# Score chain one step later, and coordinates spread by DMA instead of TensorE, in a deformable-attention kernel

## Chip, cores and metric

The kernel runs on one core of a Trainium2 chip. The metric is device time in microseconds (us) of one execution. A core has TensorE (PE; its weight loads are listed as PEld), VectorE (DVE), ScalarE (ACT), GpSimd (POOL) and a queue for DMAs (SP, SPq). They run their own instruction streams and meet at semaphores.

## What is computed

The reference applies two layers to an image x of 2 x 128 x 32 x 32. Each layer is deformable attention with 8 heads and a continuous position bias, and an MLP:

```python
q = _gconv1x1(xn, qw)
off = conv(qg, off_dw_w, stride 4, 6x6);  off = gelu(off + off_dw_b)
off = tanh(einsum(off, off_pw_w)) * OFF_SCALE
vx, vy = gx + off[:, 0], gy + off[:, 1]          # 64 sampling points per head
kv = _grid_sample(xn, (nx, ny));  k, v = _gconv1x1(kv, kw), _gconv1x1(kv, vw)
pos = grid_q[:, :, None, :] - grid_kv[:, None, :, :]
bias = sign(pos) * log1p(abs(pos))
bias = relu(bias @ cpb_w1 + cpb_b1);  bias = relu(bias @ cpb_w2 + cpb_b2)
bias = bias @ cpb_w3 + cpb_b3
attn = softmax(q @ k.T * scale + bias);  x = x + out_w @ (attn @ v) + out_b
return x + mlp_w2 @ gelu(mlp_w1 @ bn(x) + mlp_b1) + mlp_b2
```

The bias MLP runs for each of 2 x 8 x 1024 x 64 query-key pairs and is most of the work.

## The kernel before

**Tiling.** A segment is one layer of one image (4 segments). Each has 4 units (pairs of heads), a unit has two halves of the queries (32 phases in all), and a phase has 8 steps: 256 steps, 64 per segment. In a step the bias MLP is run for one slice of keys:

- VectorE makes the first hidden layer, h1 (L600, one operation over 128 x 2048, three buffers deep).
- TensorE adds the y part and the bias into PSUM ("corrections", L798, 4 products) and runs layer 2 (L824, 16 products). Both fill two of three PSUM pairs.
- ScalarE empties each pair by a relu (L452, two per step).
- TensorE runs layer 3 (L842) into the scores. In the last step of a phase the queries' product with the keys is added (L853).

**The ring.** The three PSUM pairs go round: whoever comes next takes the one that was freed first. The function `ring` settles this when the program is built. Side work that needs PSUM takes its turn too: it takes the pair of the second relu of the step before, and must wait for that relu. The next step's layer 2 then takes the pair of the side work and must wait until that is emptied. Side work that uses the ring is: q, image_t, offset, spread, sample, keys_values, scores_t, attend, project, mlp_up, mlp_down, u_rows. `max_off` writes to the scores and does not.

**What sets the order.** Tables of numbers say after which step a stage stands in the stream of its engine. On TensorE it stands behind layer 2 and before layer 3 of that step. On ScalarE it stands behind both relus. On VectorE it stands behind h1 of that step, which runs up to three steps ahead. `BEFORE_SLOTS` prepares the next segment, at steps 28 to 51 of the running one. `AFTER_SLOTS` finishes a half: attention output, projection, MLP. `SOFTMAX_SLOTS` is the chain of each phase.

**The chain of a phase.** In the step after its last one (number 1 of the next phase) ScalarE copies the scores to SBUF (`copy_scores`, L462). At 2 TensorE transposes them (`scores_t`, L932); `score_max` on VectorE (L727) takes the maxima; `widen_max` on ScalarE (L540) spreads them; `max_off` (L938) subtracts them; `exp` (L546) follows, with a table load where another function stood before.

**Preparation.** ScalarE's `conv_gelu` (step 33), TensorE's `offset` (L892) and ScalarE's tanh give offsets. `positions` on VectorE makes `coord`, with one row per key, and `pos`. Then `spread` (L901) multiplies a broadcast column of `coord` with the identity, 8 times, so that each partition has all keys' coordinates. `spread_out` on ScalarE (L509, L510) reads it into `hat_x` (as a distance) and `key_y` (a part of the tile `work`). `features` (L498 to L503) prepares the bias input. `distances` (L516, 4 pairs), `hats` and `hat_products` on VectorE and GpSimd build the bilinear weights. `sample` (L913) samples the image, and `keys_values` gives keys and values, which `keys_values_out` on ScalarE copies (L530, L532).

**SP.** SP stores the features, loads them broadcast for each unit (L368), and spreads the reciprocals of the softmax sums by a store and a broadcast load (`invert_sums`, L345), which VectorE's divide (L741) awaits.

## Time and profile before

| | us |
|---|---|
| median of 3 runs | 909.36 (906.27 to 911.7) |
| the profiled execution, whole | 908.36 |
| its span in the trace | 906.3 |
| PE busy | 814.3 |
| DVE busy | 711.1 |
| ACT busy | 675.8 |
| PE idle before the score transposes (L932) | 21.5 |

A row of the timeline gives the start, the duration, the engine, the line and the operation, with the tile written and the tiles read. In brackets stands how long the engine was idle before it, and who ended the wait. Rows of the same kind are merged (x4, x16). Matmuls are pipelined, so the last row before a wait ends a little before its modelled end. A busy TensorE is not one at its peak.

### The profile page before, as it was taken

Reading aid. Unit: us, or ns where it says so; the run is one execution under the profiler, and the core shown is the slowest. Engines: PE = TensorE matmul, PEld = TensorE weight load, DVE = VectorE, ACT = ScalarE, POOL = GpSimd, SP = SyncE. Lnnn points to the kernel's source line nnn. Section 1 sums busy time; section 2 is a strip of 40 time slices with the busy share of each in tenths; the row PEclk is TensorE's granted clock in tenths of the full one; section 3 lists DMA queues with packets and bytes.
Section 4 is the critical chain, followed back from the end, with each engine's and each line's share of the span. In section 5 each row is a group of like instructions: output and inputs, shape, how many; then the busy total and the mean of one; then the engine's idle time right before and its main releaser. Section 6 shows DMA issues by size and latency. Waiting matters only on the chain.

```text
span 906.3 us, 27727 instructions
## 1 busy us (share of the span) xinstructions
PE 814.3 (90%) x12452; PEld 229.1 (25%) x12452; DVE 711.1 (78%) x493; ACT 675.8 (75%) x773; POOL 69.1 (8%) x40
## 2 busy tenths in 40 slices
PE   3299998899999999789999999888999999999986
PEld 2122222222222222223222222222222222222222
DVE  4799798798877588888885879889887758989821
ACT  2368787978786688896876878897877768888862
POOL 2110021210000004030000001220000000000000
PEclk8589998999999999999999999999999999999999
DMA  4401010020120102002020100102011010200001
GB/s 150 95 15 48 5 31 21 8 53 4 25 44 12 50 3 50 8 3 55 2 64 14 48 4 26 27 7 54 4 34 40 8 50 2 71 5 2 2 15 36
DMA packets 23781, 27.06 MB, mean 30 GB/s; under 512 B 15600, under 2 KB 17520, under 8 KB 23664
## 3 DMA queue, kind: packets, MB, share of 16 engines
q1 hardware_dynamic: 23664, 25.29, 10.4%
q8 instruction: 99, 1.62, 0.7%
q14 instruction: 18, 0.15, 0.1%
HBM read 23.05 MB, written 2.10 MB: 28 GB/s over the span
## 4 chain that ended last, share of the span: by engine, by line
issue 58%; PE 26%; POOL 6%; ACT 5%; DVE 3%; DMA 0%; ACTq 0%; SPq 0%; POOLq 0%
PE pair L824 9%; PE scores L842 8%; POOL conv_prod L325 4%; POOL big L432 3%; ACT h L452 3%; PE pair L798 2%; DVE h L600 2%; PE pair L975 2%; PE scores L853 1%; PE pair L950 1%; PE pair L932 1%; PE pair L966 1%; ACT big L554 1%; PE scores L938 1%; ACT L554 0%
## 5 line engine op out<-in xcount | busy, mean ns | idle before, releaser
L600 DVE TENSOR_TENSOR h<-hx,hy 128x2048 f32<-128x2048 f32 x256 | 582.3, 2302 | 77.5 <-PE pair L824 73.3
L452 ACT ACTIVATE h<-pair 128x1024 f32<-128x1024 f32 x512 | 517.3, 1023 | 148.0 <-PE pair L798 104.8
L824 PE MATMUL pair<-h,wts 32*32 32x512 f32 x8192 | 301.2, 605 | 21.3 <-DVE h L600 6.7
L842 PE MATMUL scores<-h,wts 128*32 128x512 f32 x2048 | 275.7, 607 | 0.1
L798 PE MATMUL pair<-fy,u_rows 32*128 32x512 bf16 x1024 | 102.8, 388 | 16.6 <-DMA fy<-fy_dram 16.6
L824 PEld LDWEIGHTS pair<-h,wts 32*32 32x32 f32 x8192 | 66.3, 103 | 83.3 <-ACT h L452 35.3
L798 PEld LDWEIGHTS pair<-fy,u_rows 32*128 32x128 bf16 x1024 | 26.3, 91 | 234.2 <-issue 234.2
L842 PEld LDWEIGHTS scores<-h,wts 128*32 128x32 f32 x2048 | 42.1, 108 | 157.0 <-issue 148.5
L325 POOL TENSOR_TENSOR conv_prod<-qpad,wts 128x288 f32<-128x288 f32 x16 | 34.0, 2150 | 416.3 <-ACT qpad L479 416.3
L432 POOL TENSOR_TENSOR big<-big,hat_x 128x512 f32<-128x512 f32 x16 | 32.4, 2054 | 127.7 <-DVE big L698 127.7
L462 ACT ACTIVATE probs<-scores,wts 128x512 f32<-128x512 f32 x32 | 22.0, 688 | 23.8 <-PE scores L842 23.5
L932 PE MATMUL pair<-const,probs 128*128 128x128 f32 x128 | 20.1, 280 | 21.5 <-ACT h L452 20.8
L727 DVE TENSOR_REDUCE neg_max<-pair 128x8 f32<-128x512 f32 x32 | 22.1, 690 | 21.3 <-PE pair L932 21.3
L756 DVE SCALAR_TENSOR_TENSOR x<-pair,wts,x 128x512 f32<-128x512 f32 x8 | 6.0, 751 | 36.9 <-PE pair L975 36.9
L853 PE MATMUL scores<-qpad,keys_t 128*32 128x512 f32 x256 | 33.3, 592 | 0.0
L966 PE MATMUL pair<-work,wts 128*128 128x512 f32 x64 | 31.0, 612 | 1.9 <-DVE work L750 1.4
L975 PE MATMUL pair<-big,wts 128*128 128x512 f32 x64 | 29.5, 604 | 3.0 <-ACT big L554 2.9
L554 ACT ACTIVATE big<-pair,wts 128x512 f32<-128x512 f32 x32 | 20.2, 683 | 15.7 <-PE pair L966 15.6
L932 PEld LDWEIGHTS pair<-const,probs 128*128 128x128 f32 x128 | 13.4, 140 | 49.7 <-issue 48.0
L546 ACT ACTIVATE probs<-scores,wts 128x512 f32<-128x512 f32 x32 | 21.9, 685 | 3.0 <-PE scores L938 2.8
L938 PE MATMUL scores<-ident_r,neg_max_wide 128*128 128x128 f32 x128 | 22.9, 302 | 0.6 <-ACT neg_max_wide L540 0.6
L938 PEld LDWEIGHTS scores<-ident_r,neg_max_wide 128*128 128x128 f32 x128 | 17.2, 190 | 24.7 <-ACT neg_max_wide L540 16.5
(89 smaller groups left out, 358.5 us busy)
## 6 DMA issues: line engine op xcount, KB each, us to landing
hx<-features_dram SPq DMA_DIRECT2D x64, 128.0 KB, 2.8
hy<-features_dram SPq DMA_DIRECT2D x64, 128.0 KB, 3.2
att_den<-reciprocals_dram SPq DMA_DIRECT2D x8, 256.0 KB
wts<-weights_dram SPq DMA_DIRECT2D x2, 960.0 KB, 7.7
x<-x_dram SPq DMA_DIRECT2D x2, 512.0 KB, 5.5
fy<-fy_dram SPq DMA_DIRECT2D x64, 6.0 KB
fy<-fy_dram SPq DMA_DIRECT2D x64, 4.0 KB
fy<-fy_dram SPq DMA_DIRECT2D x64, 2.0 KB
```

The costliest lines, as they stand in the source:

```text
L325: return engine.tensor_tensor(out, window, taps, ALU.mult)
L432: pool.tensor_tensor(bilinear[:, k], hat_y[:, k], hat_x[:], ALU.mult).then_inc(bilinear_ready[0], 1)
L452: emptied("z", 2 * g + j, act.activation(h2[j][g % H2_BUFS][:].rearrange("p r n -> p (r n)"), pair_of("z", 2 * g + j)[:], ACT.Relu))
L600: dve.tensor_tensor(h1[g % H1_BUFS][:].rearrange("p c (y x) -> p c y x", x=W), hx[unit % 2][:, :, t].unsqueeze(2).broadcast_to([128, CT, H ...
L798: return pe.matmul(z_of(g, r), u_rows[unit // PAIRS // B][key_rows(r)], y.unsqueeze(2).broadcast_to([32, H // 2, W]), **flags)
L824: ins = pe.matmul(z_of(g, r)[32 * c:32 * (c + 1)], w(l, "w2")[key_rows(r), key_rows(r)], h1[g % H1_BUFS][key_rows(r), c], start=r >= 2, st ...
L842: ins = pe.matmul(scores[phase % 2][32 * r:32 * (r + 1)], w(l, "w3")[:, 32 * t:32 * (t + 1)], h2[rows[0] // 2][step % H2_BUFS][:, r % 2], ...
L853: ins = pe.matmul(scores[phase % 2][k], keys_t[seg % 2][:, u, k], qpad[seg % 2][:, 1 + H // 2 * h:1 + H // 2 * (h + 1), 1:W + 1], start=Fa ...
L932: ins = pe.transpose(pair_of("scores_t", phase)[:, s], probs[:, unit % PAIRS, bank(h)][:, s], cst("ident"))
L938: ins = pe.matmul(scores[phase % 2][:, 128 * k:128 * (k + 1)], neg_max_wide[:, 2 * k:2 * (k + 1)].rearrange("p n j -> p (n j)"), ident_r[: ...
L966: ins = pe.matmul(pair_of("mlp_up", n)[:, bank(k)], w(half // 2 // B, "mlp_w1")[:, 128 * c:128 * (c + 1)], xn2[:, bank(half % 2)], start=T ...
L975: ins = pe.matmul(pair_of("mlp_down", half)[:, 0:HALF], w(half // 2 // B, "mlp_w2")[:, 128 * c:128 * (c + 1)], mlp_h[:, c, bank(half % 2)] ...
```

## The change

1. In `SOFTMAX_SLOTS` and `AFTER_SLOTS` all numbers grow by one: `scores_t`, `score_max`, `widen_max`, `max_off`, `exp`, and everything that finishes a half.
2. For segments 1 to 3 `spread` and `spread_out` are gone. SP stores column 3 of `coord` (1,024 numbers of 4 bytes) to `coords_dram`, and after the store of the features it loads them back, broadcast over 128 partitions, into `hat_x` and `key_y` (256 KB each). ScalarE makes `hat_x` a distance in place (`hat_x_distance`). Segment 0 keeps the products.
3. In `BEFORE_SLOTS` offset, positions, features and features_sign move by one step, distances, hats and hat_products by three, sample, sample_out and keys_values by four. q, image_t and the convolution stay.
4. The second `u_rows` moves from step 20 to 22.

```diff
-    ("dve", "conv_sum", 1): 34, ("act", "conv_gelu", 0): 33, ("pe", "offset", 0): 35,
-    ("act", "offset_tanh", 0): 35, ("dve", "positions", 0): 38, ("pe", "spread", 0): 37,
-    ("act", "features", 0): 37, ("act", "spread_out", 0): 37, ("dve", "features_sign", 0): 40,
-    ("act", "distances", 0): 39, ("act", "distances", 1): 40, ("act", "distances", 2): 41,
+    ("dve", "conv_sum", 1): 34, ("act", "conv_gelu", 0): 33, ("pe", "offset", 0): 36,
+    ("act", "offset_tanh", 0): 36, ("dve", "positions", 0): 39, ("act", "features", 0): 38,
+    ("dve", "features_sign", 0): 41, ("act", "hat_x_distance", 0): 41, ("act", "distances", 0): 42,
...
-SOFTMAX_SLOTS = {("pe", "scores_t"): 2, ("dve", "score_max"): 4, ("act", "widen_max"): 3,
-                 ("pe", "max_off"): 4, ("act", "exp"): 4}
+SOFTMAX_SLOTS = {("pe", "scores_t"): 3, ("dve", "score_max"): 5, ("act", "widen_max"): 4,
+                 ("pe", "max_off"): 5, ("act", "exp"): 5}
...
+            def store_coords(seg):
+
+                sp.wait_ge(pos_ready, seg + 1)
+                sp.dma_start(coords_dram[seg].rearrange("n k -> k n"), coord[:, 3], allow_slow_non_contiguous=True)\
+                    .then_inc(coords_stored, 16)
+
+            def load_coords(seg):
+                for k in range(2):
+                    sp.wait_ge(bilinear_ready[k], 4 * seg)
+                sp.wait_ge(coords_stored, 16 * seg)
+                for dst, n in ((hat_x[:], 0), (key_y, PAIRS)):
+                    c = coords_dram[seg, n]
+                    sp.dma_start(dst, bass.AP(tensor=c.tensor, offset=c.offset, ap=[[0, 128], [1, 128 * PAIRS]]))\
+                        .then_inc(coords_loaded, 16)
...
                 if pair == 0:
+                    if seg:
+                        store_coords(seg)
                     store_features(seg)
+                    if seg:
+                        load_coords(seg)
                     load_features(unit)
...
+            def hat_x_distance(seg):
+
+                act.wait_ge(coords_loaded, 32 * seg)
+                act.activation(hat_x[:], hat_x[:], ACT.Abs, bias=cst("neg_x")).then_inc(hat_x_distanced, 1)
+
             def distances(n):
 
-                wait_emptied(act, "spread", n // 4)
+                if n // 4:
+                    act.wait_ge(coords_loaded, 32 * (n // 4))
+                else:
+                    wait_emptied(act, "spread", 0)
...
             def positions(seg):
                 wait_emptied(dve, "offset", seg)
+                if seg == 1:
+                    wait_filled(dve, "spread", 0)
+                if seg >= 2:
+                    dve.wait_ge(coords_stored, 16 * (seg - 1))
```

**TensorE, steps 36 and 37 of a segment's 64** (the first preparation). Before; pair0 to pair2 are the ring's pairs, h1_0 to h1_2 the hidden layer's buffers:

```order
L824 MATMUL pair1<-h1_0,wts0 32x512 x8
L824 MATMUL pair2<-h1_0,wts0 32x512 x8
L938 MATMUL scores1<-ident_r,neg_max_wide 128x128 x4
L842 MATMUL scores0<-h2_01,wts0 32x512 x2
L842 MATMUL scores0<-h2_10,wts0 32x512 x2
L798 MATMUL pair2<-fy0,u_rows0 128x512 x2
L798 MATMUL pair0<-fy0,u_rows0 128x512 x2
L824 MATMUL pair0<-h1_1,wts0 32x512 x8
L824 MATMUL pair1<-h1_1,wts0 32x512 x8
L901 MATMUL pair2<-const,coord 128x128 x8
```

After, the same two steps (layer 2 is L859, corrections L833, layer 3 L877, offset L927, max_off L973):

```order
L859 MATMUL pair1<-h1_0,wts0 32x512 x8
L859 MATMUL pair0<-h1_0,wts0 32x512 x8
L927 MATMUL pair2<-wts0,conv_act 64x8 x2
L877 MATMUL scores0<-h2_01,wts0 32x512 x2
L877 MATMUL scores0<-h2_10,wts0 32x512 x2
L833 MATMUL pair0<-fy0,u_rows0 128x512 x2
L833 MATMUL pair1<-fy0,u_rows0 128x512 x2
L859 MATMUL pair1<-h1_1,wts0 32x512 x8
L859 MATMUL pair2<-h1_1,wts0 32x512 x8
L973 MATMUL scores1<-ident_r,neg_max_wide 128x128 x4
```

The eight spread products are gone, offset has come to step 36 and max_off to step 37.

**ScalarE, around the exp with which the distances mix** (steps 42 to 44 before, 44 to 46 after). Before; big is the tile of the distances:

```order
L516 ACTIVATE big<-work,const 128x512 x2
L452 ACTIVATE h2_10<-pair0 128x1024
L452 ACTIVATE h2_01<-pair1 128x1024
L540 ACTIVATE neg_max_wide<-neg_max0 128x512
L452 ACTIVATE h2_11<-pair2 128x1024
L452 ACTIVATE h2_00<-pair0 128x1024
L546 ACT_TABLE_LOAD
L546 ACTIVATE probs<-scores0,wts0 128x512
```

After (relus are L473, distances L545, widen_max L569, exp L575):

```order
L569 ACTIVATE neg_max_wide<-neg_max0 128x512
L545 ACTIVATE big<-work,const 128x512 x2
L473 ACTIVATE h2_10<-pair0 128x1024
L473 ACTIVATE h2_01<-pair2 128x1024
L575 ACT_TABLE_LOAD
L575 ACTIVATE probs<-scores0,wts0 128x512
L545 ACTIVATE big<-work,const 128x512 x2
L473 ACTIVATE h2_11<-pair1 128x1024
L473 ACTIVATE h2_00<-pair0 128x1024
```

Before, the last distance pair stands ahead of the widening. Now the third stands behind the widening, and the fourth stands in one step with the table load and exp.

**SP, from the last loads of a segment's unit 3 to the next segment's first.** Before:

```order
L385 DMA fy1<-fy_dram 8x1x256 x4
L385 DMA fy1<-fy_dram 4x256 x4
L349 DMA features_dram<-pos_sign 128x8x32
L368 DMA hx0<-features_dram 32x1024 x4
L368 DMA hy0<-features_dram 32x1024 x4
```

After:

```order
L402 DMA fy1<-fy_dram 8x1x256 x4
L402 DMA fy1<-fy_dram 4x256 x4
L352 DMA coords_dram<-coord 128x8x1
L366 DMA features_dram<-pos_sign 128x8x32
L361 DMA hat_x<-coords_dram 128x512
L361 DMA work<-coords_dram 128x512
L385 DMA hx0<-features_dram 32x1024 x4
```

The store of the coordinates stands ahead of the features' store, and the two loads stand behind it.

## Rows read from the trace of the kernel before

**Rows 1.** The page's part 1: busy time, share of the span, instructions of each engine.
```profile
PE 814.3 (90%) x12452; PEld 229.1 (25%) x12452; DVE 711.1 (78%) x493; ACT 675.8 (75%) x773; POOL 69.1 (8%) x40
```

**Rows 2.** Groups by line: busy us, mean ns | idle before, and who ended it.
```profile
L932 PE MATMUL pair<-const,probs 128*128 128x128 f32 x128 | 20.1, 280 | 21.5 <-ACT h L452 20.8 <-ACT probs L462 0.8
```

**Rows 3.** Timeline, a plain step and a score transpose: start, us, engine, operation [idle before].
```profile
334.14 0.39 PE L798 MATMUL pair<-fy,u_rows 32*128 32x512 bf16 x4
334.57 2.11 ACT L452 ACTIVATE h<-pair 128x1024 f32<-128x1024 f32 x2 [0.31 <-PE pair L798]
336.56 0.40 PE L798 MATMUL pair<-fy,u_rows 32*128 32x512 bf16 x4
336.69 0.69 ACT L462 ACTIVATE probs<-scores,wts 128x512 f32<-128x512 f32 x1
337.28 1.93 ACT L452 ACTIVATE h<-pair 128x1024 f32<-128x1024 f32 x2
338.44 0.63 PE L932 MATMUL pair<-const,probs 128*128 128x128 f32 x4 [0.39 <-ACT h L452]
```

**Rows 4.** Timeline, steps 34 to 38 of the second stretch of preparation.
```profile
363.66 1.92 ACT L452 ACTIVATE h<-pair 128x1024 f32<-128x1024 f32 x2
364.81 0.63 PE L932 MATMUL pair<-const,probs 128*128 128x128 f32 x4 [2.04 <-ACT h L452]
...
366.54 0.69 DVE L727 TENSOR_REDUCE neg_max<-pair 128x8 f32<-128x512 f32 x1
...
372.37 1.28 ACT L546 ACT_TABLE_LOAD   x1
...
375.41 2.02 PE L901 MATMUL pair<-const,coord 128*128 128x128 f32 x16 [1.11 <-ACT h L452]
376.06 0.43 ACT L498 ACTIVATE pos_abs<-pos 128x256 f32<-128x256 f32 x1
...
378.56 0.67 ACT L509 ACTIVATE hat_x<-pair,const 128x512 f32<-128x512 f32 x1
...
379.77 1.15 PE L824 MATMUL pair<-h,wts 32*32 32x512 f32 x32 [1.02 <-ACT work L510]
```

**Rows 5.** Stretches from one step's start to another's: length, busy time per engine, granted clock.
```profile
361.27:369.58 8.31, 5.75 (x101) 1.64 (x98) 8.31 (x6) 6.40 (x9) 0.00 (x0) 1.00 0.01 3
361.27:387.56 26.29, 21.44 (x348) 6.84 (x345) 23.03 (x23) 23.23 (x30) 0.00 (x0) 1.00 0.04 7
387.56:410.64 23.08, 19.27 (x328) 4.88 (x325) 21.71 (x16) 20.27 (x25) 7.87 (x4) 1.00 0.09 26
```

**Rows 6.** Timeline, steps 42 and 47 of the same stretch of preparation.
```profile
391.18 1.35 ACT L516 ACTIVATE big<-work,const 128x512 f32<-128x512 f32 x2
393.58 0.63 PE L932 MATMUL pair<-const,probs 128*128 128x128 f32 x4 [1.65 <-ACT h L452]
...
407.70 1.15 PE L824 MATMUL pair<-h,wts 32*32 32x512 f32 x32 [0.93 <-DVE h L600]
```

**Rows 7.** Timeline, step 52: layer 2 behind the copies of keys and values.
```profile
425.58 1.15 PE L824 MATMUL pair<-h,wts 32*32 32x512 f32 x32 [0.84 <-ACT values L532]
```

**Rows 8.** Timeline, the tail: the spread reciprocals and who awaits them.
```profile
870.59 0.62 SPq L345 DMA_DIRECT2D att_den<-reciprocals_dram  x1
874.05 0.69 DVE L741 TENSOR_TENSOR work<-att_sum,att_den 128x512 f32<-128x512 f32 x1 [5.00 <-DMA att_den<-reciprocals_dram]
876.67 0.69 DVE L727 TENSOR_REDUCE neg_max<-pair 128x8 f32<-128x512 f32 x1 [1.92 <-PE pair L932]
```

**Rows 9.** DMA issues by line, and all transfers of features_dram, issue to landing.
```profile
features_dram<-pos_sign SPq DMA_DIRECT2D x4, 128.0 KB, 2.3
...
DMA to landing us min/median/max: 2.2/3.0/6.6
```

**Rows 10.** Stretches: steps 35 and 36 in the first and the second segment.
```profile
149.14:157.90 8.76, 8.33 (x101) 2.00 (x98) 8.25 (x12) 5.07 (x7) 0.00 (x0) 0.63 0.01 3
366.37:372.81 6.44, 5.76 (x102) 1.73 (x99) 6.27 (x10) 5.05 (x7) 0.00 (x0) 1.00 0.01 3
```

30 lines of the change are left out of this document (18 added, 12 removed).

## The prediction

> **What bounds the kernel now.** I read the page's busy shares first [rows 1]: TensorE is busy 90% of the span, VectorE 78%, ScalarE 75%. Then I laid TensorE's rows out by step, one step being the stretch from one start of L798 to the next. A step without side work takes 2.42 us (334.14 to 336.56 in [rows 3]). Two relus need 2.11 us of it and one h1 operation 2.3 us of VectorE. So TensorE sets the pace, but with only 0.3 us of slack on ScalarE: any extra activation puts ScalarE ahead of TensorE as the bound for a few steps. Back to back, relus follow each other at 0.91 us instead (1.93 for two in [rows 3]), so a late ScalarE catches up at most 0.6 us a step.
>
> I number steps within a segment's 64. Those that matter are 34 to 56, where the next segment is prepared; in the second such stretch of the trace step 34 starts at 361.27.
>
> **The chain one step later, plain phases.** TensorE waits 20.8 us in all before the score transposes L932, always for a relu [rows 2]. There are 31 waits: three of 2.04, three of 1.65 ([rows 4, 6] show one of each), and 25 of 0.39, of which [rows 3] shows one. Why 0.39: L932 takes the buffer of the last relu of the step before. That relu could start 0.43 after the step's start (334.57), but L462 has ScalarE from 336.69 and the relus start at 337.28, which is 0.72 after the step's start. One step later L462 is long done. What is left: 0.43 + 1.02 + 0.13 hand-over (363.66 + 1.02 to 364.81) = 1.58, against 1.49 at which TensorE is ready (1.88 less 0.39): 0.09. Saved 0.30 each. In 6 of the 25 phases mlp_down now moves into the very step after L462 and inherits the wait; they give nothing. 19 x 0.30 = **5.7 us**.
>
> **Steps 34 to 40.** Here ScalarE is late and I follow it from the rows [rows 4], time 0 at the start of step 34; [rows 5] has the lengths of whole stretches.
> - Before: the first relu after conv_gelu ends at 3.41 (363.66 + 1.02), L932 runs behind it, step 36 starts at 8.31.
> - After: layer 3 of step 34 (1.0) runs inside that wait. Step 35's corrections wait until 3.5, its layer 2 until the next relu at 4.4, L932 follows at 5.5 without a wait, and step 36 starts at 7.1.
> - The offset product (0.3) is now in step 36. Layer 2 of step 36 needs the buffer that score_max empties. VectorE did that at 366.54 behind two h1; now a third h1 (2.3) stands ahead, so it ends at about 8.2: a wait of 0.8. Step 37 starts at 10.7.
> - Steps 37 to 40 before: L901 2.02 with 1.11 waited, then 1.02 for L510. After: no L901, L509 or L510, but max_off (0.6). ScalarE does a table load and exp (1.28 at 372.37, and 0.6 as L462 takes at 336.69) in step 37 and features (2.50, 376.06 to 378.56) in step 38. These 4.4 us exceed its slack: TensorE waits about 0.1, 0.7, 0.5 and 0.6 in steps 39 and 40. Step 41 starts at 23.8.
> - Before, step 41 starts at 26.29. Saved **2.5 us** a segment. The 4.2 us that the deleted work cost is not all won, since ScalarE is the bound and loses only 1.26.
>
> **Steps 41 to 47.** The four distance pairs (1.2 each, 1.35 with the overlap to the next relu) move three steps. Now ScalarE has L462 and the new hat_x_distance in 41 (0.6 + 0.6), a pair in 42 and 43, widen and a pair in 44, and in 45 load, exp and a pair, 3.1 us in one step. By the same walk TensorE waits 0.6 before layer 2 of 43, 1.0 before L932, 0.5 in 46, 2.0 before the corrections of 47 and 0.7 behind them: 4.8. With 7 x 2.42, L932, max_off and L853 (2.1 together) that is 23.8, against 23.08 before [rows 5], which held 1.65 for L932 and two waits for h1, the longer one 0.93 [rows 6]. Those two go, because hats and products move later while TensorE waits for ScalarE. Lost **0.7 us** a segment.
>
> **Steps 48 to 56.** The sample product moves from 48 to 52 at the same cost. keys_values moves to 55, the step that has L853, and its copies no longer stand behind a widen; layer 2 no longer waits 0.84 for them [rows 7]. Saved **0.8 us** a segment.
>
> **Edits at nothing.** The max_off next to q, the projections and L966 only shifts. The waits of 0.3 to 0.4 for L554 at the first mlp_up are hidden by L853 now, and come back at about 0.3 after the second. The u_rows product leaves the step of max_off and gains 0.3, once. In the tail, attend of half 6 is one step (2.42) later; its divide, which waits for the DMA until 874.05, then comes at 876.5 and pushes score_max from 876.67 to 877.2: **0.6 us** lost [rows 8].
>
> **The DMAs.** SP's queue gets one store (1,024 elements of 4 bytes) and two broadcast loads of 256 KB per segment. Nothing else on SP is due then: the next loads wait for h1 of step 47. The nearest row of the store is the store of the features, 128 KB in 1,024 pieces: 2.3 us to landing, and no transfer of that tensor, loads included, took over 6.6 [rows 9]. It is issued at about 15 on my scale, the loads at 21, behind the features store: 5 to 6 us of cover. The nearest row of a load is att_den: 3.46 us from issue (870.59) to the divide that awaits it (874.05) [rows 8]. The second load is issued 0.6 later, so both have landed at 25.1. hat_x_distance comes up on ScalarE at 26.9. Cover 1.8 us, price nothing. At the upper bound of 6.6 they land at 28.2, 1.3 late, 3.9 us over three segments. The lower bound is zero too; a load cannot gain.
>
> A rule speaks against the store. The features store, in pieces of 128 bytes, landed 2.3 us after its issue [rows 9]. The Trainium skill, page DMA: Bandwidth & Descriptors, section Specifications, says that transfers under 512 bytes miss the line rate because the DMA engine reads, modifies and writes. No row here shows pieces of 4 bytes. By the row the sum is as below; by the rule the store lands later, and the sum is the same until it has used up its 5 us of cover, so the rule only raises the chance of the late rival.
>
> **Sum.** 5.7 + 3 x (2.5 - 0.7 + 0.8) + 0.3 - 0.6 = 13.2 us. The profiled execution took 908.36 (span 906.3 and 2.1 around it): 895.2. The median before, 909.36, lies 1.0 higher, so I forecast **896.2**.
>
> **The clock.** Steps 35 and 36 of the first segment, behind the first 2.04 wait, ran at a mean granted clock of 0.63 and took 8.76 us; those of the second, behind an equal wait, ran at 1.00 and took 6.44 [rows 10]. 0.63 is a mixture of the two levels, 1.2 and 2.4 GHz, and the dip cost 2.3 us. I count one dip after as well. None would be 2.3 less; one in each segment 4.6 more.
>
> **Rivals.**
> - ScalarE's backlog dissolves faster than my walk says, and the deleted L901 and both its waits count in full (4.2 instead of 2.5, no 0.7 lost): 896.2 - 3 x 2.4 = 889.0. For it: ScalarE's mean load is 75%. Against: L932 at 2.04 and 1.65 shows it saturated here. Chance 0.08.
> - The 0.39 waits stay, because the relu is bound by its own product and not by L462: 896.2 + 5.7 = 901.9. Against: the 0.43 and 0.72 above. Chance 0.10.
> - Clock dips behind the new 2.0 wait of step 47, up to three in all: 896.2 + 4.6 = 900.8, with 1 or 2 us of waits that I missed 903. Chance 0.13.
> - Slower than before: the coordinates land late. hat_x_distance then holds ScalarE, already the bound, with all relus behind it, and TensorE behind them, in three segments. It costs 3 us for each us beyond the cover of 1.8, so it takes back the whole gain from a landing 10.5 us after the first load's issue instead of 4.1, and at 12.5 gives 916. Nothing in the rows takes over 6.6. Chance 0.05.
> - The change doesn't do what it says: ScalarE's burst in step 45 costs what the spread gave, and h1 gets late again; phases 4 to 6 gain nothing (+7.8) and half of the plain gain is passed on to other steps (+3): 906 to 907. Chance 0.06.
> - The forecast, 891 to 900: chance 0.58.
>
> **How the numbers follow.** The range takes in the first three rivals, 889 to 903.5, and leaves out the rest. Half a per cent, 4.5 us, is about what a measurement can tell from no change. Faster by more (under 904.8): the forecast and the first three, less a margin for waits that a walk misses, 0.85. Within it: 0.09. Slower: the late landing and a margin, 0.06.
>
> **What would show it.** Right: L932's wait is 0.1 in plain phases and its total about 5; L975 shows six waits of 0.4; the L901 group has 16 instructions; step 41 starts about 24 us behind step 34; ScalarE waits for no DMA before hat_x_distance. Wrong: a wait of ScalarE for coords_dram, DVE h waits in steps 46 to 51, or a stretch from step 34 to step 48 that is no shorter than 49.4 us. The step I trust least is the walk through ScalarE's backlog.

## The result and the profile after

The changed kernel is slower: 917.52 us (median of 6 runs, 915.26 to 919.18) against 909.52 us (6 runs, 906.27 to 912.19) on the same chip, a ratio of 1.0082 with a 95% interval of 1.0056 to 1.0108. The forecast was 896.2 us. The profiled execution took 917.28 us, with a span of 915.4.

In the changed kernel's numbering h1 is L630, the score transposes are L967 (L932 before), score_max is L762, hat_x_distance L536, and SyncE's wait for the coordinate store L358.

The page's part 1, first line, against [rows 1]:

```profile
PE 827.2 (90%) x12404; PEld 228.3 (25%) x12404; DVE 718.9 (79%) x493; ACT 675.3 (74%) x770; POOL 66.3 (7%) x40
```

TensorE has 48 products fewer and yet is busy 12.9 us longer than the 814.3 of before. The same work runs slower; the clock is where to look. The mean granted clock is 0.965, where it was 0.979.

The score transposes, the line that the chain was moved for, against [rows 2]; first the group of the line, then the waits of layer 2 and of the corrections that are new or have grown (engine, line, who was waited for: us in total, times, longest):

```profile
L967 PE MATMUL pair<-const,probs 128*128 128x128 f32 x128 | 20.9, 287 | 6.7 <-ACT h L473 3.2
```

```profile
PE pair L859 <- ACT h L473: 11.2, 22, 0.6
PE pair L833 <- ACT h L473: 9.7, 9, 1.7
PE pair L859 <- DVE neg_max L762: 8.6, 7, 3.1
```

The waits before the score transposes fell from 21.5 to 6.7 us, near the forecast of about 5. In their place stand waits that were 3.9 us (layer 2 for a relu), nothing (the corrections for a relu) and 1.5 us in 3 (layer 2 for a maximum) before.

SyncE's wait for the coordinate store (same columns), and how long transfers took from issue to landing (the last number of an issue's line, the median in us):

```profile
SPq L358 <- DMA coords_dram<-coord: 9.7, 3, 3.9
```

```profile
hat_x<-coords_dram SPq DMA_DIRECT2D x3, 256.0 KB, 3.1
work<-coords_dram SPq DMA_DIRECT2D x3, 256.0 KB, 4.0
features_dram<-pos_sign SPq DMA_DIRECT2D x4, 128.0 KB, 5.1
```

The timeline of SyncE's issues in the second preparation shows the store issued at 380.05 and the first load at 390.70, right after SyncE has seen the store's completion:

```profile
380.05 0.40 SPq L352 DMA_DIRECT2D coords_dram<-coord  x1
386.32 0.39 SPq L366 DMA_DIRECT2D features_dram<-pos_sign  x1
390.70 0.34 SPq L361 DMA_DIRECT2D hat_x<-coords_dram  x1
391.08 0.43 SPq L361 DMA_DIRECT2D work<-coords_dram  x1
```

So the store landed 10.6 us after its issue (8.7 to 10.6 us in the three segments), and the features behind it took 5.1 us where [rows 9] has 2.3. The loads themselves took 3.1 to 5.9 us, not far from the 3.46 of the forecast; it is their issue that came late. The transfer's packets were done long before. The stretch from 379.9 to 391 us in 40 slices shows the DMA engines busy in slices 5 to 7 (381.0 to 381.8) and then idle until the features:

```profile
DMA  0000771000000000000000003048860000000000
GB/s 0 0 0 0 7 7 1 0 0 0 0 0 0 0 0 0 0 0 0 0 0 0 0 0 59 0 69 138 137 100 6 12 11 0 0 0 0 0 0 0
```

What followed on ScalarE and TensorE in steps 41 to 43 and at step 47 (timelines: start, us, engine, operation, idle before and releaser):

```profile
394.99 0.72 ACT L536 ACTIVATE hat_x<-hat_x,const 128x512 f32<-128x512 f32 x1 [1.95 <-DMA work<-coords_dram]
```

```profile
396.68 0.39 PE L833 MATMUL pair<-fy,u_rows 32*128 32x512 bf16 x2 [1.59 <-ACT h L473]
397.59 1.15 PE L859 MATMUL pair<-h,wts 32*32 32x512 f32 x32 [0.52 <-ACT h L473]
399.81 0.83 PE L967 MATMUL pair<-const,probs 128*128 128x128 f32 x4 [1.07 <-ACT h L473]
...
413.19 0.39 PE L833 MATMUL pair<-fy,u_rows 32*128 32x512 bf16 x2 [1.66 <-ACT h L473]
414.11 2.02 PE L859 MATMUL pair<-h,wts 32*32 32x512 f32 x32 [0.52 <-ACT h L473]
```

The last row's layer 2 takes 2.02 us instead of 1.15: behind the wait the clock has fallen. The stretches of the changed kernel, against [rows 5]; columns as there (length, busy time of PE, PEld, DVE, ACT, POOL, granted clock, DMA): first steps 34 to 40 in the second preparation and steps 41 to 47 in all three, then three of the stretches at the low level:

```profile
367.11:389.80 22.69, 20.37 (x332) 5.32 (x330) 20.20 (x22) 20.72 (x26) 0.00 (x0) 1.00 0.07 8
173.16:202.01 28.85, 24.38 (x329) 5.66 (x327) 23.21 (x16) 22.11 (x27) 10.12 (x4) 0.82 0.23 60
389.80:418.44 28.64, 22.94 (x330) 5.37 (x327) 23.99 (x15) 22.24 (x28) 9.98 (x4) 0.88 0.25 61
607.17:633.42 26.25, 21.46 (x328) 5.17 (x325) 23.44 (x14) 22.11 (x27) 11.91 (x4) 0.93 0.27 65
```

```profile
127.20:134.10 6.90, 5.79 (x40) 1.62 (x44) 5.54 (x4) 1.54 (x2) 0.00 (x0) 0.52 0.05 8
...
400.30:403.70 3.40, 3.40 (x37) 0.62 (x44) 3.02 (x3) 2.11 (x4) 0.00 (x0) 0.53 0.00 0
414.00:417.40 3.40, 3.29 (x40) 0.69 (x44) 3.40 (x3) 1.99 (x3) 1.23 (x1) 0.54 0.02 5
```

A granted clock near 0.5 is the level of 1.2 GHz. Behind the start of the kernel, the trace of before has one such stretch (149.0 to 155.8 us); this one has seven: at 127, 182, 199, 400, 414, 629 and 902 us.

One loss is neither a wait nor the clock. Layer 2 of step 40 takes 2.01 us in the first preparation and 2.15 in the third, at a granted clock of 1.00, where the second has 1.15 (two timeline rows, then the stretch of the first, columns as above):

```profile
170.22 2.01 PE L859 MATMUL pair<-h,wts 32*32 32x512 f32 x32 [0.52 <-ACT h L473]
387.71 1.15 PE L859 MATMUL pair<-h,wts 32*32 32x512 f32 x32 [0.52 <-ACT h L473]
...
170.22:172.16 1.94, 1.94 (x32) 0.60 (x32) 1.94 (x1) 0.99 (x2) 0.00 (x0) 1.00 0.20 32
```

It starts 7.7 us behind the issue of the store (162.55). Four of the five traces with the 4-byte store show it, in two preparations each, with 1.9 to 3.1 us, and none of the other traces of this study does. So the store seems to reach TensorE's own products too, by a way that no view shows. It is why steps 34 to 40 are about 1 us longer in the first and third preparation (23.55 and 23.70 us) than in the second (22.69).

The last new wait is in step 28 of the first segment, where VectorE has hidden terms, norm1, another h1 and only then the maximum:

```profile
128.31 2.02 PE L859 MATMUL pair<-h,wts 32*32 32x512 f32 x32 [3.09 <-DVE neg_max L762]
```

Laid out by step, the two traces differ so (us, changed minus before, in the profiled executions; segments 0 to 2 hold the three preparations):

| steps | segment 0 | 1 | 2 | 3 |
|---|---|---|---|---|
| 0 to 27 | -0.98 | +0.46 | +0.46 | +0.46 |
| 28 to 33 | +5.93 | +0.70 | +0.69 | 0.00 |
| 34 to 40 | -5.19 | -3.60 | -2.61 | -0.22 |
| 41 to 47 | +5.79 | +5.56 | +3.19 | -0.21 |
| 48 to 55 | -1.37 | -1.42 | -0.46 | -0.22 |
| 56 to 63 | -0.20 | -0.22 | -0.22 | -0.23 |

The entry of -5.19 holds 2.4 us of clock: the one fall of the trace of before lies there. The start adds 0.7 us and the tail 2.4 (32.72 us from the last segment's end where 30.37 stood, 1.7 of it L1001 at the low clock). The start is no effect of the change: in the later traces of the kernel before with idle copies, whose start is the same code, step 0 comes 0.2 and 1.0 us later than in the trace of before.

### The profile page after: what moved, and what is told of

Same layout as the page of the kernel before. It is cut to its first block, busy times and chain, and to the rows that moved or that the text cites. A ratio compares the mean times of both kernels' runs of the same rounds, so it can differ in the third digit from the quotient of the medians.

```text
span 915.4 us, 27640 instructions
## 1 busy us (share of the span) xinstructions
PE 827.2 (90%) x12404; PEld 228.3 (25%) x12404; DVE 718.9 (79%) x493; ACT 675.3 (74%) x770; POOL 66.3 (7%) x40
## 4 chain that ended last, share of the span: by engine, by line
PE 66%; ACT 10%; DVE 10%; DMA 7%; issue 6%; SPq 1%; POOL 0%; ACTq 0%; DVEq 0%; POOLq 0%
PE pair L859 23%; PE scores L877 19%; PE pair L833 6%; ACT h L473 5%; DVE h L630 5%; DMA coords_dram<-coord 3%; PE pair L1010 3%; PE pair L1001 3%; PE scores L888 3%; PE pair L967 2%; PE pair L985 2%; DMA work<-coords_dram 2%; PE scores L973 1%; PE pair L912 1%; ACT big L545 1%
## 5 line engine op out<-in xcount | busy, mean ns | idle before, releaser
L630 DVE TENSOR_TENSOR h<-hx,hy 128x2048 f32<-128x2048 f32 x256 | 587.6, 2319 | 75.1 <-PE pair L859 71.0
L473 ACT ACTIVATE h<-pair 128x1024 f32<-128x1024 f32 x512 | 516.0, 1023 | 171.8 <-PE pair L833 123.1
L859 PE MATMUL pair<-h,wts 32*32 32x512 f32 x8192 | 306.0, 612 | 20.7 <-ACT h L473 11.2
L877 PE MATMUL scores<-h,wts 128*32 128x512 f32 x2048 | 280.3, 613 | 0.1
L833 PE MATMUL pair<-fy,u_rows 32*128 32x512 bf16 x1024 | 107.6, 388 | 27.3 <-DMA fy<-fy_dram 17.5
L833 PEld LDWEIGHTS pair<-fy,u_rows 32*128 32x128 bf16 x1024 | 27.5, 91 | 250.2 <-issue 236.7
L859 PEld LDWEIGHTS pair<-h,wts 32*32 32x32 f32 x8192 | 66.9, 104 | 84.1 <-ACT h L473 42.4
L877 PEld LDWEIGHTS scores<-h,wts 128*32 128x32 f32 x2048 | 43.9, 108 | 160.2 <-issue 154.8
L453 POOL TENSOR_TENSOR big<-big,hat_x 128x512 f32<-128x512 f32 x16 | 40.9, 2587 | 164.6 <-DVE big L733 164.6
L327 POOL TENSOR_TENSOR conv_prod<-qpad,wts 128x288 f32<-128x288 f32 x16 | 22.6, 1443 | 402.1 <-ACT qpad L500 402.1
L1001 PE MATMUL pair<-work,wts 128*128 128x512 f32 x64 | 32.6, 639 | 2.5 <-DVE work L785 1.4
L762 DVE TENSOR_REDUCE neg_max<-pair 128x8 f32<-128x512 f32 x32 | 22.0, 686 | 14.6 <-PE pair L967 14.6
L967 PE MATMUL pair<-const,probs 128*128 128x128 f32 x128 | 20.9, 287 | 6.7 <-ACT h L473 3.2
L575 ACT ACTIVATE probs<-scores,wts 128x512 f32<-128x512 f32 x32 | 21.9, 685 | 3.0 <-PE scores L973 2.8
L973 PEld LDWEIGHTS scores<-ident_r,neg_max_wide 128*128 128x128 f32 x128 | 17.2, 190 | 24.8 <-ACT neg_max_wide L569 13.5
L973 PE MATMUL scores<-ident_r,neg_max_wide 128*128 128x128 f32 x128 | 23.0, 302 | 0.1
L967 PEld LDWEIGHTS pair<-const,probs 128*128 128x128 f32 x128 | 13.8, 143 | 34.7 <-issue 33.0
```

The source lines that it names most:

```text
L327: return engine.tensor_tensor(out, window, taps, ALU.mult)
L453: pool.tensor_tensor(bilinear[:, k], hat_y[:, k], hat_x[:], ALU.mult).then_inc(bilinear_ready[0], 1)
L473: emptied("z", 2 * g + j, act.activation(h2[j][g % H2_BUFS][:].rearrange("p r n -> p (r n)"), pair_of("z", 2 * g + j)[:], ACT.Relu))
L630: dve.tensor_tensor(h1[g % H1_BUFS][:].rearrange("p c (y x) -> p c y x", x=W), hx[unit % 2][:, :, t].unsqueeze(2).broadcast_to([128, CT, H ...
L833: return pe.matmul(z_of(g, r), u_rows[unit // PAIRS // B][key_rows(r)], y.unsqueeze(2).broadcast_to([32, H // 2, W]), **flags)
L859: ins = pe.matmul(z_of(g, r)[32 * c:32 * (c + 1)], w(l, "w2")[key_rows(r), key_rows(r)], h1[g % H1_BUFS][key_rows(r), c], start=r >= 2, st ...
```

## The experiments

Four theories stood after the comparison. **T1**: the store lands late, ScalarE and TensorE pay for it. **T2**: VectorE's order, in which the maxima, one step later, now stand behind the hidden terms (slot 12 of a unit), norm1 (28) and `fy_weights` (23). **T3**: ScalarE has too much in step 45 (table load, exponential and the last pair of distances), hence the waits of 1.66 and 0.52 us at step 47. **T4**: the clock falls behind the longer waits, and that is a price of its own. All ratios are against runs of the kernel before on the same chip; the changed kernel's is 1.0082 [1.0056, 1.0108].

### Spread by TensorE in the changed kernel's timetable

```diff
-    ("act", "hat_x_distance", 0): 41,
+    ("pe", "spread", 0): 38, ("act", "spread_out", 0): 38,
```

> The changed kernel's timetable, chain one step later included, but the coordinates of segments 1 to 3 are spread by TensorE products at step 38 and taken out by ScalarE there, as before; no coordinate store or load. Against the changed kernel only the transfer is undone. Theory T1 (the store of the coordinates lands about 10 us after its issue, ScalarE then stands still in hat_x_distance for 1.0 to 1.9 us, the features behind the store come later, and TensorE pays in steps 41 to 48): hat_x_distance's three waits of 4.0 us and the late features go, minus some 2.5 us for the second preparation's spread in steps 34 to 40 (2.5 x 3 = 7.5 us was what the walk put on it): 917.5 - 3 x 3 + 7.5, about 914 to 917, and the stretch between steps 41 and 48 falls from 28 to about 24 or 25 us. Theory T2 (VectorE's order: the score maxima stand behind the hidden terms and norm1) leaves the waits of layer 2 on the maxima at 8.6 us in 7, as in the changed kernel; if it alone is the loss, then 917.5 + 7.5 = 925. Theory T3 (ScalarE's load in step 45): the wait of 1.66 us at step 47 stays.

Measured: 913.78 us, ratio 1.0062 [1.0039, 1.0084]. The stretch of steps 41 to 47 came down to 25.64, 23.05 and 24.71 us (with a fall of the clock in the first and the third), and steps 34 to 40 went up to 25.22. The two waits of step 47 (1.66 and 0.52) stayed, and so did layer 2's waits for the maxima (10.2 us in 8). So the transfer is not the whole loss: without it the kernel is still 0.6% slower than before.

### The transfer with the old chain

```diff
-SOFTMAX_SLOTS = {("pe", "scores_t"): 3, ("dve", "score_max"): 5, ("act", "widen_max"): 4,
-                 ("pe", "max_off"): 5, ("act", "exp"): 5}
+SOFTMAX_SLOTS = {("pe", "scores_t"): 2, ("dve", "score_max"): 4, ("act", "widen_max"): 3,
+                 ("pe", "max_off"): 4, ("act", "exp"): 4}
```

(and `AFTER_SLOTS` one step earlier likewise)

> The changed kernel's transfer of the coordinates and its later preparation, but the softmax chain in the steps of before. T1: the transfer's loss stays whole and the plain phases lose their gain of 19 x 0.22 = 4.2 us: 921 to 922 us. T2: the waits of layer 2 on the score maxima (8.6 us in 7, and about 2.3 us of lower clock behind the longest) go, so 917.5 + 4.2 - 10.9 = 911 us. T4 (the clock falls behind each longer wait): with fewer waits at most four low stretches instead of seven.

Measured: 919.67 us, ratio 1.0123 [1.0108, 1.0138]: T1's side. The later chain looks like a gain of some 0.4% in this surrounding (the two intervals just touch, at 1.0108), so the loss comes mainly from the other half of the change. The clock has five low stretches behind the start, where T4 allowed four. T2's picture was too simple: layer 2 waits for a maximum here as well, 9.0 us in 6, the longest 3.05 at step 51, behind the hat products that the later preparation moved there.

### VectorE's order, first attempt

```diff
-    ("dve", "norm1", 0): 28, ("pe", "q", 0): 28, ("act", "q_out", 0): 28,
+    ("dve", "norm1", 0): 29, ("pe", "q", 0): 29, ("act", "q_out", 0): 29,
-TERMS_SLOT = 12
+TERMS_SLOT = 13
```

> The changed kernel with VectorE's order mended: the hidden terms at slot 13 instead of 12 and norm1, q and its taking out at 29 instead of 28, so that each score maximum stands ahead of them as before. T2: the seven waits of layer 2 on the maxima (3.1, 0.49, 0.48, three times 1.15, 1.06; 8.6 us) go, and with them the lower clock of 127 to 134 us (2.3 us): 907 us. T1 alone: those waits are not what costs, or come back elsewhere (q and the hidden terms one step later make others wait): 915 to 918 us. Coordinates' transfer as in the changed kernel, so steps 41 to 48 stay at 26 to 29 us.

Measured: 918.09 us, ratio 1.0107 [1.0086, 1.0128]: T2's 907 missed. Steps 28 to 33 of the first segment fell from +5.93 to +1.04 and steps 0 to 27 of the second from +0.46 to -0.76, as T2 said. But layer 2 still waits 8.7 us in 6 for maxima, now at other steps (1.54 at step 36 of the second preparation), and step 43 there has a wait of 2.93 us before the corrections (1.59 in the changed kernel). What the start of each segment gave, its preparation took back.

### Loads that wait for nothing, the store kept

```diff
-                sp.wait_ge(coords_stored, 16 * seg)
-                    c = coords_dram[seg, n]
+                    c = x_in[0, n]
```

> The changed kernel, but the coordinate loads don't wait for the store and read the first rows of the input instead of the coordinates (the coordinates of segments 1 to 3 are left out of the computation; the store is still made). T1: ScalarE's waits for the loads (4.0 us in 3, longest 1.95) go, and since SP no longer stands for the store's landing nothing else waits for it; what stays is the features behind the store. The stretch between steps 41 and 48 falls by 1 to 2 us in each segment and one or two dips of the clock with it: 917.5 - 3 x 1.5 - 2 = 911 us. T3 (ScalarE's load, exp and last distances in step 45 make the wait at step 47, not the transfer): 1.66 us at step 47 stays in all three segments and the time is 916 to 917. T2: unchanged, 917.

Measured: 914.13 us, ratio 1.0071 [1.0054, 1.0088]. The loads read the input instead of the coordinates, which are left out. In the second preparation they were issued at 382.39 and 384.27, right behind the features, and landed only at 389.11 and 390.46, 6.7 and 6.2 us later:

```profile
390.49 0.72 ACT L535 ACTIVATE hat_x<-hat_x,const 128x512 f32<-128x512 f32 x1 [1.87 <-DMA work<-x_dram]
```

The store at 375.61 is 14.9 us back by then. In the first and third preparation the loads took 4.4 to 4.8 us and ScalarE waited for none. The features behind the store took 4.7 to 4.9 us in all three. So SyncE's waiting alone is not the price: what stands behind the store in the queue is late too, the features always, the loads in one preparation of three.

### No store at all

```diff
-                        store_coords(seg)
```

(with the free loads of the last kernel)

> The changed kernel without the coordinate store, its loads free of any wait and reading the first rows of the input (the coordinates of segments 1 to 3 are left out of the computation). Theory T1a: in the run where the loads were freed but the store stayed, they still landed 6.2 to 6.7 us after issue, because the store of 4-byte pieces ahead of them in the same queue held them; without it they land 3 to 4 us after issue, ScalarE's hat_x_distance doesn't wait, the features land 2.3 us after issue, and step 43 (7.7 us in the changed kernel's second segment) falls to the 4.0 us of the TensorE spread: ratio 1.003 to 1.005 where the freed loads gave 1.007. T3: the waits of 1.66 us at step 47 stay all the same. If the store isn't the cause the loads again land after 6 us.

Measured: 907.62 us, ratio 0.9989 [0.9971, 1.0008]. T1a holds: the features land 2.3 us after issue again, the loads take 4.1 to 4.9 us in all three preparations, ScalarE waits for none, step 43 takes 4.61 us instead of 7.74, and the kernel is 0.9% faster than the changed one. The 1.66 us of step 47 are still there in all three segments: they are not the transfer's.

### The store in pieces of 32 bytes

```diff
-                sp.dma_start(coords_dram[seg].rearrange("n k -> k n"), coord[:, 3], ...)
+                c = coords_dram[seg]
+                sp.dma_start(bass.AP(tensor=c.tensor, offset=c.offset, ap=[[2 * PAIRS, 128], [1, 2 * PAIRS]]), coord[:, 3])
```

> The changed kernel, but the store writes each partition's eight coordinates as one piece of 32 bytes (128 pieces instead of 1024 of 4 bytes). The loads are as before and so read the coordinates in the wrong order (a permutation; sampling falls in other places, with the same work). Theory T1b (the late landing comes from the many 4-byte pieces): the store lands in 2 to 4 us instead of 8.7 to 10.6, SyncE's wait for it (9.7 us in 3) nearly goes, and the ratio comes to that of the kernel without a store, 0.999 to 1.001. If any store behind a wait for another engine lands that late, whatever its pieces, the ratio stays 1.008.

Measured: 907.42 us, ratio 0.9986 [0.9965, 1.0007]. Issue to landing, same columns as above:

```profile
hat_x<-coords_dram SPq DMA_DIRECT2D x3, 256.0 KB, 3.5
work<-coords_dram SPq DMA_DIRECT2D x3, 256.0 KB, 3.9
features_dram<-pos_sign SPq DMA_DIRECT2D x4, 128.0 KB, 2.3
coords_dram<-coord SPq DMA_DIRECT2D x3, 4.0 KB, 1.4
```

The same 4 KB from the same tile to the same tensor, in 128 pieces instead of 1,024, land 1.4 us after issue (2.6 in the first segment) instead of 8.7 to 10.6. The number of pieces alone is not the cause, since the features store has 1,024 as well, of 128 bytes, and lands after 2.3 us [rows 9]. So the late landing comes from storing single 4-byte elements. They also go out in transposed order, which the 32-byte pieces do not (the loads then read the coordinates in a wrong order); no run separates the size from the order. SyncE's wait for the store is gone from its list of waits.

### The store by rows, with the right coordinates

```diff
-                ordered(dve.tensor_scalar(coord[:, 3], coord[:, 1], -0.5, None, ALU.add))
+                ordered(dve.tensor_scalar(coord_out[:, 0:2 * PAIRS], coord[:, 1], -0.5, None, ALU.add))
+                if seg:
+                    ordered(dve.transpose(coord_rows[:], coord_out[:]))
...
+                sp.dma_start(bass.AP(tensor=c.tensor, offset=c.offset, ap=[[32, 4], [128, 32], [1, 32]]), coord_rows[:])
```

VectorE transposes the 32x32 blocks of a [128, 32] tile whose first 8 columns are the coordinates; the store writes 128 rows of 128 bytes into a tensor with 32 rows a segment, of which the loads read the first 8 as before.

> The changed kernel with the right coordinates, stored in pieces of 128 bytes: VectorE turns its 32x32 blocks first (one more small instruction on VectorE in the positions, an estimate of 0.2 us three times), the store then has 128 pieces of 128 bytes, 16 KB; the loads are unchanged. T1b: it lands in 2 to 4 us and the time is that of the kernel without a store plus under 1 us: ratio 0.999 to 1.002, faster than the changed kernel by 6 to 8 us. Otherwise 1.008.

Measured: 907.69 us, ratio 0.9999 [0.9981, 1.0018]. The transposing instruction:

```profile
L683 DVE STREAM_TRANSPOSE coord_rows<-coord_out x3: 211/211/213, 161.1 to 589.1; 128x32 f32<-128x32 f32 x3
```

It takes 0.21 us, and the 0.8% are back. The loads are issued 6.5 us after the store and SyncE no longer waits for it; when exactly it lands, the trace does not show. The three stretches of its second preparation, steps 34 to 40, 41 to 47 and 48 to 55:

```profile
362.81:385.51 22.70, 20.37 (x332) 5.32 (x328) 20.41 (x23) 20.74 (x26) 0.00 (x0) 1.00 0.10 26
385.51:410.77 25.26, 21.23 (x328) 5.08 (x325) 24.18 (x14) 22.15 (x28) 12.02 (x4) 0.93 0.22 53
410.77:435.88 25.11, 23.99 (x440) 7.65 (x438) 23.20 (x15) 19.20 (x24) 0.00 (x0) 1.00 0.02 4
```

73.07 us in all, against 75.11 before (26.29 and 23.08 of [rows 5], and 25.74), and with one stretch at the low clock in it. That is the gain that the forecast gave this part (2.6 us a segment, here 2.0), and the kernel as a whole is still only level with before. So 8 us of the miss were the store, and the rest lies elsewhere.

This kernel and the first experiment's have the same timetable and differ only in who spreads the coordinates. With TensorE's spread the same three stretches take 74.99 us, 1.9 more, and the kernel's ratio is 1.0062 against 0.9999, with intervals that don't meet. In this timetable the transfer is worth 0.6%, once its store lands early.

### The last pair of distances at 47

```diff
-    ("act", "distances", 3): 45
+    ("act", "distances", 3): 47
```

> The changed kernel with the last pair of distances at step 47 instead of 45, out of the exponential's step. T3: the wait of corrections at step 47 (1.66 us, three times) and layer 2's 0.52 us behind it go or shrink to under 0.5 us each, the stretch between steps 41 and 48 falls by 2 to 3 us in each segment, a new wait of hats at 48 on the distances costs VectorE up to 1 us: 917.5 - 3 x 2.2 + 1, about 911 to 913, ratio 1.001 to 1.004. T1 alone (the wait at 47 comes from the late loads): it only moves, and the ratio stays 1.008.

Measured: 918.61 us, ratio 1.0121 [1.0089, 1.0152]. T3's mechanism is there: the wait before the corrections of step 47 fell from 1.66 to 0.44. Its price is not: steps 49 to 52 took over with waits for h1 (1.28, 0.93, 0.88) and a maximum (1.85), since hats and products came later, and steps 48 to 55 went from -1.4 to +3.4.

### Everything exactly one step later, spread by TensorE

```diff
-    ("act", "distances", 0): 42, ("act", "distances", 1): 43, ("act", "distances", 2): 44, ("act", "distances", 3): 45
+    ("act", "distances", 0): 40, ("act", "distances", 1): 41, ("act", "distances", 2): 42, ("act", "distances", 3): 43
```

(hats, products, sample, keys and values likewise one step behind the kernel before, TensorE's spread at 38)

> The spread on TensorE as before, the chain one step later as in the changed kernel, and the whole second preparation from the offset product on exactly one step later than before (distances at 40 to 43 instead of 42 to 45), so that no pair of distances shares a step with the exponential at 45. Theory T3 (the pair of distances in the exponential's step makes the waits of 1.66 and 0.52 us at step 47, and the waits of step 43 come from distances pressed against the copy at 42): against the timetable of the changed kernel with TensorE's spread (1.0062 of before) those waits go, 3 x 2.2 us, and a low stretch or two of the clock with them: 906 to 909 us, ratio 0.998 to 1.001. Theory T2 (VectorE: fy_weights and norm1 ahead of a maximum at step 28 of segment 0, 3.1 us and a low clock behind it; hidden terms ahead of a maximum, 1.15 us three times) leaves these where they were. If T3 is wrong the ratio stays near 1.006.

Measured: 911.95 us, ratio 1.0036 [1.0018, 1.0054]. The wait of 1.66 us at step 47 is gone (the 0.52 behind it stays), and steps 41 to 47 take 22.4 us in each segment, 0.6 less than before; steps 48 to 55 take 0.6 more. 0.3% better than the timetable of the change, where 0.5 to 0.8% were expected.

### TensorE's spread, everything one step later, VectorE's order mended

```diff
-TERMS_SLOT = 12
+TERMS_SLOT = 13
-    put("pe", 22, "u_rows", 1)
-    put("dve", 23, "fy_weights", 1)
+    put("pe", 19, "u_rows", 1)
+    put("dve", 20, "fy_weights", 1)
```

> TensorE's spread, everything from offset on one step later, u_rows and fy_weights at steps 19 and 20 instead of 22 and 23, hidden terms at 13 instead of 12: the chain's gain without the collisions that the runs showed. T2: the wait of 3.1 us at step 28 of segment 0 falls under 1 us and its low clock goes, the three waits of 1.15 us at step 12 go (4.6 to 8 us less than the kernel that is sent beside it with the late fy_weights and early terms). Plain phases keep 19 x 0.22 = 4.2 us of gain: 899 to 903 us, ratio 0.990 to 0.995, faster than before. If the loss lies elsewhere, both kernels have the same time.

Measured: 908.05 us, ratio 0.9993 [0.9975, 1.0011], where 0.990 to 0.995 was expected; against the same kernel with the old order (1.0036, same chip) that is 0.4% less. The 3.1 us of step 28 and the three waits of 1.15 us went, but `fy_weights` now stood in front of a maximum. There VectorE first waits 3.0 us for the `u_rows` product and then works 2.6 us on it (102.14 to 104.76), before it can go on with h1 and the maximum:

```profile
107.62 1.15 PE L824 MATMUL pair<-h,wts 32*32 32x512 f32 x32 [2.93 <-DVE neg_max L727]
```

The place for it is directly behind a maximum, 22.

### Store by rows, distances at 41 to 44

```diff
-    ("act", "distances", 0): 42, ("act", "distances", 1): 43, ("act", "distances", 2): 44, ("act", "distances", 3): 45
+    ("act", "distances", 0): 41, ("act", "distances", 1): 42, ("act", "distances", 2): 43, ("act", "distances", 3): 44
```

(hats 45 and 47, sample 50, keys and values 53)

> The kernel that stores by rows, with the distances at steps 41 to 44 instead of 42 to 45 and all that follows from hats on one to two steps earlier (hats 45 and 47, sample 50, keys and values 53), so that no distances share the exponential's step 45. T3: the waits of 1.66 us at step 47 and of 1.85 us at step 52 (a maximum behind VectorE's late hat products) shrink as they did with the preparation one step later (41 to 56: -0.6 + 0.6 against +0.6 + 1.0 us per segment): 3 x 1.5 = 4 us less than the kernel beside it, ratio 0.994 to 0.997. Against it: ScalarE has hat_x_distance and a pair of distances in one step, 41, and the copy at 42, so the wait of 1.07 us at step 43 may double; then no difference.

Measured: 909.34 us, ratio 1.0002 [0.9984, 1.0020], no difference from 0.9999. The wait at step 47 fell from 1.66 to 0.44 and step 43 rose from 4.61 to 7.16 us (0.75 before the corrections, 0.52, 1.07, and a low clock behind them). The objection in the expectation decided it.

### Store by rows, distances at 41 to 44, VectorE's order mended

```diff
-TERMS_SLOT = 12
+TERMS_SLOT = 13
-    put("pe", 22, "u_rows", 1)
-    put("dve", 23, "fy_weights", 1)
+    put("pe", 20, "u_rows", 1)
+    put("dve", 22, "fy_weights", 1)
```

> As the one with rows and earlier distances, and VectorE's order mended where it cost: hidden terms at 13 instead of 12, u_rows and fy_weights at 20 and 22 instead of 22 and 23 (fy_weights behind the maximum of step 21, further from norm1 and the maximum of 29). T2: three waits of 1.15 us go, the 3.1 us at step 28 of segment 0 falls under 1.5 us, some 0.8 us per segment comes back in steps 41 to 48: 3.5 + 2 + 2 (its low clock) - 2.4, about 5 us less than the kernel beside it: ratio 0.988 to 0.992, faster than before by 7 to 11 us. If the order was not the cause, both have one time.

Measured: 904.93 us, ratio 0.9950 [0.9932, 0.9969], 0.5% faster than before, and 0.5% faster than the kernel beside it; 0.988 to 0.992 was expected. Layer 2 no longer waits for any maximum; what it waits for now:

```profile
PE pair L866 <- ACT h L476: 11.2, 22, 0.6
...
PE pair L866 <- DVE h L633: 6.8, 7, 2.0
PE pair L840 <- ACT h L476: 5.3, 9, 0.8
```

The step tables of the two kernels show where the expected 5 us came from: steps 0 to 33 gave 9.6 us over the four segments (5.2 of them in the first), and steps 41 to 55 took 4.4 back, where VectorE's h1 comes later.

### Store by rows, mended order, the change's own distances

The edits to VectorE's order above, on the kernel that stores by rows, with the distances at 42 to 45.

> The changed kernel with the store by rows and VectorE's mended order, the distances where the change has them (42 to 45). T3 (the pair in the exponential's step costs): slower than the best kernel's 0.995 by the 1 to 2 us it was thought to be worth, 0.996 to 0.997. What the two kernels without the mended order showed (0.9999 with the distances at 42 to 45, 1.0002 with 41 to 44) speaks for no difference: ScalarE has too much work in these steps wherever the distances stand, and the wait only moves; then 0.995.

Measured: 906.75 us, ratio 0.9962 [0.9945, 0.9979], against 0.9999 without the mended order. With 0.9950 for the distances at 41 to 44 the intervals overlap: whether their slots cost a tenth of a per cent stays open, a whole per cent they don't. The order is not wholly mended here: layer 2 still waits 5.5 us in 3 for maxima, behind the later hat products.

### TensorE's spread with the mended order

The kernel one step later throughout, with `u_rows` at 20, `fy_weights` at 22 and the hidden terms at 13.

> The best kernel's chain and its mended order of VectorE (hidden terms at 13, u_rows and fy_weights at 20 and 22), but the coordinates spread by TensorE and the preparation exactly one step later than before. It tells what the transfer itself is worth once the store lands early. T2 says the mended order gives again what it gave between the two kernels with a store by rows (0.0052): 1.0036 - 0.0052, ratio 0.998. Then the transfer is worth 3 us (0.995 against 0.998). If the ratio is 0.993 or lower, the transfer costs even when its store lands early, and the chain alone is the gain.

Measured: 903.58 us, ratio 0.9932 [0.9908, 0.9956], the fastest kernel of the study. Against the same kernel with the old order (1.0036) the mending gave 1.0%, twice what was expected. Its second preparation, the same three stretches:

```profile
357.78:383.00 25.22, 21.88 (x349) 7.02 (x346) 21.61 (x22) 22.04 (x28) 0.00 (x0) 1.00 0.04 7
383.00:406.20 23.20, 19.70 (x328) 4.97 (x326) 21.16 (x14) 21.37 (x27) 7.87 (x4) 1.00 0.09 26
406.20:432.71 26.51, 24.16 (x440) 7.68 (x437) 24.01 (x15) 19.20 (x24) 0.00 (x0) 1.00 0.13 27
```

| second preparation, us | 34 to 40 | 41 to 47 | 48 to 55 | sum |
|---|---|---|---|---|
| before | 26.29 | 23.08 | 25.74 | 75.11 |
| changed | 22.69 | 28.64 | 24.32 | 75.65 |
| store by rows | 22.70 | 25.26 | 25.11 | 73.07 |
| store by rows, distances 41 to 44, mended order | 22.70 | 25.19 | 27.21 | 75.10 |
| TensorE's spread, mended order | 25.22 | 23.20 | 26.51 | 74.93 |

With the mended order the transfer saves 2.5 us in steps 34 to 40, and all of it is gone by step 56. The kernels with it have 0.9950 and 0.9962, the one without 0.9932. The intervals against before overlap, but the last two ran on the same chip: 902.11 to 905.13 us without the transfer, 905.54 to 908.17 with it, no run in common. The expectation called a ratio of 0.993 or lower a sign that the transfer costs even when its store lands early; the measured one stands at that bound. It is not the transfer alone, though. In one and the same timetable, with the old order, it gained 0.6% (above). TensorE's spread lets the distances start two steps earlier (40 instead of 42), and that goes with this kernel as well; no run takes the two apart under the mended order. A part of the difference comes from the clock: 0.968 in the one profile, 0.979 in the other, and the kernel with the transfer has four stretches at the low level behind its start where the other has one.

### Idle ScalarE work in a quiet stretch of the kernel before

```diff
+                if g % SEG_STEPS == 24:
+                    for _ in range(3):
+                        ordered(act.activation(pad[:].rearrange("p (a b) -> p a b", a=4),
+                                               cst("ident").unsqueeze(1).broadcast_to([128, 4, 128]), ACT.Copy))
```

and the same with `range(6)`.

> The kernel before, with three more ScalarE copies (128x512, about 0.6 us each) into an unused buffer at step 24 of each of the four segments, in a stretch where nothing else goes on. They make TensorE wait once in each segment. Theory T4a (a wait costs its own length and no more): 3 x 0.6 less ScalarE's slack of some 0.4 us a step, 1.0 to 1.8 us four times: 4 to 7 us, ratio 1.004 to 1.008, and the granted clock stays at 1.00 there. T4b (a wait of 1 to 2 us lets the clock fall behind it): up to four low stretches of 3.4 us, each 1.7 us more, ratio 1.012 to 1.015.

> The same with six copies each time (3.6 us of ScalarE). T4a: 2.5 to 3.6 us four times, 10 to 14 us, ratio 1.011 to 1.016. T4b: low stretches behind each of them, 7 us more, ratio 1.019 to 1.024. Beside the kernel with three copies it shows from which length of wait the clock falls.

Measured: three copies 914.48 us, ratio 1.0057 [1.0039, 1.0076]; six copies 924.11 us, ratio 1.0146 [1.0105, 1.0186]. With three, TensorE waits 0.27, 0.52 and 0.43 us, 1.22 in all, in each of the four places; with six it waits 2.25 and 0.53. The granted clock in the 3.4 us behind the waits, first with three copies (the second and the last place), then with six (the first, the second and the last):

```profile
340.60:344.00 3.40, 3.37 (x52) 1.09 (x56) 2.70 (x4) 2.12 (x3) 0.00 (x0) 1.00 0.00 0
...
774.40:777.80 3.40, 3.40 (x54) 0.68 (x52) 3.18 (x4) 2.12 (x3) 0.00 (x0) 1.00 0.02 5
```

```profile
123.30:126.70 3.40, 3.40 (x40) 1.14 (x44) 0.36 (x1) 2.40 (x3) 0.00 (x0) 0.50 0.00 0
...
341.50:344.90 3.40, 2.88 (x38) 1.00 (x36) 0.00 (x0) 2.78 (x4) 0.00 (x0) 0.54 0.00 0
...
782.00:785.40 3.40, 2.88 (x38) 1.00 (x36) 0.00 (x0) 2.78 (x4) 0.00 (x0) 0.52 0.00 0
```

Behind 1.2 us of waits the clock stayed at 2.4 GHz, four times of four; behind 2.8 us it fell to 1.2, four times of four. A fall costs here 3.4 us at half speed, 1.7 us. So T4b holds for the long waits and T4a for the short ones. The profiled executions add up by that. With three copies step 26 takes 4.71 us instead of 3.44, 1.27 more; four times that is 5.1, and the span is 912.0 - 906.3 = 5.7 longer. With six it takes 7.55 to 7.78 (119.68 to 127.46 in the first segment), 4.1 to 4.3 more, of which 2.4 are waits and 1.7 the clock; the four make 16.9, and the span is 16.8 longer. By its time alone the six-copy kernel would not decide: 1.0146 lies in T4a's 1.011 to 1.016, below T4b's 1.019 to 1.024. The granted clock decides, and the waits came out shorter than the 2.5 to 3.6 us assumed.

Between the two lengths the traces show both outcomes. In the four traces with the old chain (before, three copies, six copies, the transfer with the old chain) the clock fell behind the 2.04 us before the score transposes of step 34 five times of twelve. Behind the 1.65 us of step 42, which three of them have, it fell once of nine.

## Why the prediction was wrong

**The sign came from three things, none of them in the sum.**

- *The store's price.* The step that failed is "5 to 6 us of cover" and the "price nothing" that follows from it, with the upper bound of 6.6 us. The nearest row of the store was taken to be the features store, by its 1,024 pieces; but those are of 128 bytes. In the place of 2.3 to 6.6 us stood 8.7 to 10.6. The chain that the late rival described is what happened (ScalarE held in hat_x_distance by 1.05, 1.95 and 1.04 us, relus behind it, TensorE behind them), but its price, 3 us for each us late, counted only ScalarE's delay: by it these waits, 4.0 us in all, cost 4.0, and the runs put 8 on the store. It left out that the features behind the store would be late too, that layer 2 of step 40 would be held for about 1 us twice, and that each wait could lower the clock. The late rival's chance of 0.05 was too small, given that the text itself named a kind of piece that no row showed. The rule that it cited, from the Trainium skill, DMA: Bandwidth & Descriptors, section Specifications (under 512 bytes a transfer misses the line rate through read-modify-write), pointed in the right direction, but it does not separate the cases: pieces of 32 bytes, equally under 512, landed in 1.4 to 2.6 us here, and the features' pieces of 128 bytes in 2.3. Corrected, this term is 8 us by the runs (1.0082 against 0.9989 without a store, 0.9986 with 32-byte pieces).
- *VectorE's order.* The step that failed is "Edits at nothing", which moved the maxima one step without asking what stands at that slot. VectorE has 2.3 us of h1 in each step of 2.42, so whatever it must do first (0.8 us of norm1, 1.5 of hidden terms, 2.6 of `fy_weights` and the wait for its product, or one more h1) is paid by TensorE when layer 2 needs the buffer that the maximum empties. The trace after has 8.6 us of such waits. The runs put the mended order at 0.4% (0.9999 to 0.9962), 0.5% (1.0002 to 0.9950) and 1.0% (1.0036 to 0.9932) in three surroundings; in the first the two intervals just don't meet, and the first and the third pair compare ratios from different chips. One attempt, which also moved norm1 and q, gave nothing; what in it did so was not taken apart.
- *The clock.* "I count one dip after as well" against seven. The rival for it was there with 0.13 and up to three dips, at step 47 only; those three came (199, 414, 629 us), and four more elsewhere. TensorE's busy time is 12.9 us longer with less work, and the span times (1 - mean clock) gives 32.0 us lost to the low clock in the changed kernel, 19.0 before, 18.9 in the fastest kernel. In one execution each, and part of it while TensorE was not what all waited for, this is a size and no exact price; but it is why the kernel is slower although TensorE's idle time fell, from 92.0 to 88.2 us. The experiment with idle copies shows the fall as the wait's consequence.

**What is left.** Forecast and result are 21.3 us apart. The runs put 8 of them on the store and 3 to 5 on VectorE's order, and the plain phases' term was 1.5 too large. The remaining 7 to 9 us are not taken apart. The kernel that stores by rows has a mean clock of 0.970, which by the same reckoning is 27.1 us lost against 19.0 before, so much of it may be the clock; no run shows that.

**Right, point by point.** The score transposes' wait fell to nothing in plain phases and its total to 6.7 (forecast about 5); mlp_down's six waits are 0.29 (0.4). A plain phase saves 0.22 us where the term had 0.30: the transposes' step went from 3.44 to 3.15, but the step before it from 2.42 to 2.48, so the term is 19 x 0.22 = 4.2 instead of 5.7 us. The walk through steps 34 to 40 gave 23.8 us; measured 23.55, 22.69 and 23.70, and 22.70 in all three where the store was early, so the 2.5 us were 3.6. On the way step 35's corrections came at 3.44 (3.5), its layer 2 at 4.35 (4.4) and step 36 at 7.03 (7.1). The wait of 0.8 behind the third h1 did not come. The burst of step 45 was forecast with waits of 2.0 and 0.7 at step 47 and came with 1.66 and 0.52, in every kernel that had it. Steps 48 to 55 gave 1.4, 1.4 and 0.5 (0.8).

**Where the expected gain of the transfer went.** The forecast booked +2.5 - 0.7 + 0.8 a segment. With the store mended the first term of that sum is even larger, 3.6, and steps 41 to 47 take 2.2 back (25.26 against 23.08), so the walk was about right in sum, and 2.0 us a preparation stay (75.11 to 73.07). But ScalarE, not TensorE, is the bound there: three sets of slots for the distances only moved the waits between steps 43, 47 and 49 to 52. With VectorE's order mended, what was won by taking TensorE's work away was given back within 20 steps (75.10).

The tail's 0.6 us came as 0.59 (30.96 us in the kernel that stores by rows, 30.37 before); the changed kernel's 2.4 has a fall of the clock in it.

**The later chain** seems to be a gain, as forecast. Together with VectorE's mended order and a preparation that is one step later, and without the transfer, it makes the kernel 0.7% faster (0.9932). The chain by itself was not run against the kernel before; the pair that isolates it, inside the change, gives 0.4% (1.0123 to 1.0082).

## What to carry to other kernels

Price a small transfer by its piece size and order, not by its bytes or by its piece count alone, and write it in rows: one 0.21 us transpose on VectorE took away SyncE's waits for a store (9.7 us in 3) and gave back 0.8% of the kernel. When a whole chain moves by a step, list for each engine what its new slot holds ahead of it: an engine that is 95% full in its steps (2.3 us of 2.42) makes every extra operation ahead of a late-read result a wait of the bound. And count waits of TensorE from about 2 us on at more than their length: the clock fell behind 2.8 us each time, and behind 2.04 us in some of the cases.

## What the runs showed of the hardware

- A store from SBUF to DRAM of 4 KB in 1,024 pieces of 4 bytes had its packets done within about 2 us and signalled its completion 8.7 to 10.6 us after issue; in 128 pieces of 32 bytes it landed in 1.4 us (2.6 once). What the remaining 8 us are, after the last packet, no view here shows.
- It also held what came behind it in the same queue: a features store of 128 KB took 5.1 us instead of 2.3. Two loads of 256 KB that depended on nothing took 6.7 and 6.2 us in one preparation of three, and 4.4 to 4.8 in the others, where without the store they took 4.1 to 4.9.
- In four of the five traces with that store, a layer 2 of TensorE about 7 us behind its issue took 1.9 to 3.1 us instead of 1.15, at a granted clock of 1.00 and with no wait in it, in two preparations each; in no trace without the store. By what way, no view shows.
- TensorE's granted clock stayed at 2.4 GHz behind waits of 1.2 us in all and fell to 1.2 GHz behind 2.8 us, in eight places of eight. Between these lengths it may go either way: it fell behind five of twelve waits of 2.04 us ([rows 10] shows one of each kind) and behind one of nine of 1.65 us.
- VectorE's transpose of 32x32 blocks over a 128x32 tile took 0.21 us.
